# A selective-scan and mixture-of-experts kernel: one tile in four is added into y by a DMA instead of by GpSimd

## The chip, the cores and the metric

The kernel runs on one core of a Trainium2 chip. The time is the device time of one launch in microseconds (us); lower is better. Three runs of the kernel before gave 4412.04, 4418.58 and 4423.32 us, so the median is 4418.58 us.

## The reference, cut to what matters

`x` has the shape (8, 1024, 256). Eight batches go through a bidirectional Mamba block (512 channels, 16 states per channel) and a mixture of experts, each with layer norms and a residual. The change touches the sum over the states:

```
dA = exp(delta[..., None] * A)
bx = delta[..., None] * Bm[:, :, None, :] * x[..., None]
def step(h, inp):
    dAi, bxi, ci = inp
    h = dAi * h + bxi
    return (h, jnp.einsum('ben,bn->be', h, ci))
y = jnp.transpose(ys, (1, 0, 2)) + Dp * x
```

For each time step and channel, `y` is a sum over 16 states `n` of `h_n * c_n`, in each direction, and the two directions are added.

## The kernel before, in words

There are 16 passes `w` (8 batches, two directions), each with 16 states `n`. Per state the kernel handles 4 units of 128 channels x 1024 time steps. For each unit GpSimd makes the drive (`feed_drive`, line 1895, a product of 128x1024), ScalarE makes the decay in two halves of 128x512 (`feed_decay`, line 1610), and VectorE runs two scans of 128x512 into `h` (`scan`, lines 1393 and 1396; line 1384 in the last pass). There are three places for drives and three for decays. GpSimd waits at the semaphore `scanned` until VectorE has emptied the place that it writes next, and can thus be up to three units ahead.

After the four units of a state, TensorE turns `h` into 8 tiles of 128 time steps x 512 channels (`turn_tile`, line 1170, four transposes each) in one of three PSUM buffers `h_t`. A tile `i` is then multiplied by its column of C and summed into `y[:, tb, :]`, where `tb` is its number from 0 to 7. Two ways exist:

- VectorE does both in one instruction (`sum_tile`, line 1405): 1488 tiles.
- ScalarE scales it, and GpSimd adds it. `by_pool` picks the tiles whose number modulo 16 is 2, 6, 10 or 14, one in four. ScalarE writes one of two buffers `scaled` (`scale_tile`, line 1631) and GpSimd adds the buffer into `y` (`pool_tile`, line 1913): 496 tiles. Their `tb` is always 2 or 6, so these two tiles of `y` are only ever touched by ScalarE and GpSimd during a batch.

The first 8 tiles of a batch are written straight into `y` by ScalarE (64 in all), once the DMA that dumps this tile of the batch before (`y_dump`, line 2157, issued by SyncE) has landed. In the last pass the work is cut into two halves of 512 time steps: there 4 tiles per state are summed, so one and the same tile of `y` (first 6, then 2) gets every adding.

The order on each engine is fixed. Time is counted in slots, two per unit; in slot `s` the engines handle their share of a unit, then the tile `s - 8` (GpSimd: `s - 9`), then side work (projections, convolution, norms, experts) from the table `AT`. Side work of GpSimd: `u_mul` (line 1924, 64 products of 128x1024), small norm steps, and in each batch 16 scattering DMAs (line 1970) and 16 gathering DMAs (line 1982), which GpSimd issues itself. All other DMAs are issued by SyncE.

Of the kernel before, what the change touches and what calls it, by code (L numbers as in the profile page):

```python
# [9 lines left out]
ALU = mybir.AluOpType  # L10
# [16 lines left out]
N_SCALED = 2  # L27
# [503 lines left out]
class Plan:  # L531
# [23 lines left out]
    def nth(self, piece, *index):  # L555
        return self.at[piece, index]
# [151 lines left out]
def mamba_moe(nc, x, w_in_t, chan, wx_t, wdt_t, w_out_t, router_w, router_b, w1, b1_t, w2, b2, out):  # L708
# [65 lines left out]
    with ctx:  # L774
        def sb(name, shape):
            return ctx.enter_context(nc.sbuf_tensor(name, shape, F32))

        def sem(name):
            return ctx.enter_context(nc.semaphore(name))
# [23 lines left out]
        scaled = sb("scaled", [P, N_SCALED, ED])  # L803
        conv_diag = sb("conv_diag", [P, TAPS, P])
        y = sb("y", [P, TB, ED])
# [108 lines left out]
        zeros_set = sem("zeros_set")  # L914
        zeros_out = sem("zeros_out")
        tile_scaled = sem("tile_scaled")
        gathered = sem("gathered")
        b_row_in = [sem(f"b_row_in{i}") for i in range(N_B_ROW)]
        y_dumped = [sem(f"y_dumped{i}") for i in range(TB)]
        ew_in = [sem(f"ew_in{i}") for i in range(N_EW + len(wide))]  # L920
# [100 lines left out]
        def state_of(i):  # L1021

            if i < SPLIT * TILES:
                gn, tb = divmod(i, TB)
                return (*divmod(gn, N), tb)
            hs, q = divmod(i - SPLIT * TILES, QB)
            part, n = divmod(hs, N)
            return SPLIT, n, (NH - 1 - part) * QB + q
# [11 lines left out]
        def is_first(i):  # L1040

            return i % (2 * TILES) < TB

        def by_pool(i):
            return i % (2 * TB) in POOL_TILES or is_first(i)

        of_vector = list(accumulate(not by_pool(i) for i in range(NW * TILES)))
        of_pool = list(accumulate(by_pool(i) and not is_first(i) for i in range(NW * TILES)))

        def summed_to(i):  # L1050

            return of_vector[i]

        def pooled_to(i):

            return i + 1 - summed_to(i)

        def gathered_to(i):

            return of_pool[i]  # L1060

        def wait_y(engine, i):

            if i < SPLIT * TILES:
                wait_tile(engine, i - TB)
            elif state_of(i)[1] or i < SPLIT * TILES + QB:
                wait_tile(engine, i - QB)
            else:
                wait_tile(engine, SPLIT * TILES - TB + state_of(i)[2])

        def wait_tile(engine, before):

            if not by_pool(before):
                engine.wait_ge(summed, summed_to(before))
            elif is_first(before):
                engine.wait_ge(tile_scaled, pooled_to(before))
            else:
                engine.wait_ge(gathered, gathered_to(before))

        def ew_place(i):  # L1080

# [271 lines left out]
        def dve_program(dve):  # L1353
# [44 lines left out]
            def sum_tile(i):  # L1398
                w, n, tb = state_of(i)
                b, d = divmod(w, 2)  # L1400
                c_n = c_col[:, w % 2, tb, n:n + 1]
                dve.wait_ge(turned, i + 1)
                dve.wait_ge(done["c_copy"], nth("c_copy", w, NH - 1))
                wait_y(dve, i)
                dve.e.scalar_tensor_tensor(out=y[:, tb, :], in0=h_t[i % N_H_T][:, :], scalar=c_n,  # L1405
                                           in1=y[:, tb, :], op0=ALU.mult, op1=ALU.add).then_inc(summed, 1)
# [186 lines left out]
        def act_program(act):  # L1593
# [23 lines left out]
            def scale_tile(i):  # L1617
                w, n, tb = state_of(i)
                b, d = divmod(w, 2)
                at = gathered_to(i) - 1  # L1620
                act.wait_ge(turned, i + 1)
                act.wait_ge(done["c_copy"], nth("c_copy", w, NH - 1))
                if is_first(i):
                    if b:
                        act.wait_ge(y_dumped[tb], 16 * b)
                    into = y[:, tb, :]
                else:
                    if at >= N_SCALED:
                        act.wait_ge(gathered, at - N_SCALED + 1)
                    into = scaled[:, at % N_SCALED, :]  # L1630
                act.e.mul(into, h_t[i % N_H_T][:, :], c_col[:, w % 2, tb, n:n + 1]).then_inc(tile_scaled, 1)  # L1631

# [239 lines left out]
            for s in range(plan.first, plan.end):  # L1872
                if 0 <= s + N_DECAY - 1 < NH * NU:
                    feed_decay(s + N_DECAY - 1)
                hs, into = divmod(s - 2 * WHOLE - 5, 2 * EC // NH)
                if not into and 0 <= hs < N:
                    keep_h(hs)
                i = s - 2 * EC
                if 0 <= i < NW * TILES and by_pool(i):
                    scale_tile(i)  # L1880
                for piece, index in plan.of("act", s):
                    side_piece(piece, index)


        def pool_program(pool):
# [22 lines left out]
            def pool_tile(i):  # L1908
                tb = state_of(i)[2]
                at = gathered_to(i) - 1  # L1910
                pool.wait_ge(tile_scaled, pooled_to(i))
                wait_y(pool, i)
                pool.e.tensor_tensor(y[:, tb, :], y[:, tb, :], scaled[:, at % N_SCALED, :], ALU.add  # L1913
                                     ).then_inc(gathered, 1)

            def side_piece(piece, index):
                if piece == "u_mul":
# [107 lines left out]
            for s in range(plan.first, plan.end):  # L2025
                k, odd = divmod(s, 2)
                if not odd and 0 <= k + 2 < NU:
                    feed_drive(k + 2)
                i = s - 2 * EC - 1
                if 0 <= i < NW * TILES and by_pool(i) and not is_first(i):  # L2030
                    pool_tile(i)
                for piece, index in plan.of("pool", s):
                    side_piece(piece, index)


        def sp_program(sp):
# [269 lines left out]
            sp.wait_ge(scattered, 16 * TOP * TB * NB)  # L2306
            for k in range(2):
                sp.wait_ge(x_out[k], 16 * NB)
            for tb in range(TB):
                sp.wait_ge(y_dumped[tb], 16 * (NB - 1))  # L2310

# [2 lines left out]
        act_program(Waiter(nc.scalar))  # L2314
        pool_program(Waiter(nc.gpsimd))
        sp_program(Waiter(nc.sync))


# [35 lines left out]
```

## Time and profile before

| | |
|---|---|
| median of 3 runs | 4418.58 us |
| lowest, highest | 4412.04, 4423.32 us |
| span of the profiled execution | 4422.2 us |
| VectorE busy | 3788.5 us (86%) |
| TensorE busy | 3604.0 us (81%) |
| GpSimd busy | 3504.8 us (79%) |
| ScalarE busy | 3101.8 us (70%) |
| bytes moved by DMA | 705.06 MB |

The page gives the profiled execution by its span, from the first to the last instruction; it lies within the three timed runs. An engine counts as busy while an instruction works; issuing a DMA counts as busy on GpSimd in the rows of lines 1970 and 1982, not on SyncE. Groups name the line of the program, the engine, the output and the inputs; "idle before" is the time in which the engine stood still just before them, with what ended it.

### The profile page before, as it was taken

The numbers are of one execution on the slowest core, as the hardware profiler recorded it, in microseconds if no ns is written. First come the engines' busy times: TensorE is split into PE (matmuls) and PEld (weight loads), VectorE is DVE, ScalarE is ACT, GpSimd is POOL, SyncE is SP. The second block draws the span as 40 slices with busy tenths as digits, with TensorE's granted clock in tenths as the row PEclk, the third lists the DMA queues.
The fourth block names the chain that finished last, engine by engine and source line by source line (L and its number), as shares of the span: only waits on it lengthen the run. The fifth ranks groups of instructions, "written<-read, shape, count | busy, mean of one in ns | idle before, by whom it ended". The sixth has DMA issues, their size and how long they took to land.

```text
span 4422.2 us, 57941 instructions
## 1 busy us (share of the span) xinstructions
PE 3604.0 (81%) x18192; PEld 2562.9 (58%) x18192; DVE 3788.5 (86%) x4688; ACT 3101.8 (70%) x5179; POOL 3504.8 (79%) x2085
## 2 busy tenths in 40 slices
PE   4767596888879887798878887798987989788877
PEld 1444454666546655567555774556655665567656
DVE  3999999898998989899898988989999898989710
ACT  4667576787767876688766887678876787668543
POOL 3898887888878888788887888878887888878611
PEclk7878697999979999899879998899998999889988
DMA  6233142556435663357433674345743565336555
GB/s 196 91 107 104 69 150 75 191 183 214 155 104 172 205 210 130 105 182 245 153 124 131 197 238 147 125 151 194 230 141 107 179 220 188 130 113 204 167 167 182
DMA packets 375805, 705.06 MB, mean 159 GB/s; under 512 B 31937, under 2 KB 205514, under 8 KB 371530
## 3 DMA queue, kind: packets, MB, share of 16 engines
q1 hardware_dynamic: 363210, 667.79, 46.0%
q0 software_dynamic: 12288, 33.57, 2.3%
q8 instruction: 145, 2.38, 0.2%
q14 instruction: 162, 1.33, 0.1%
HBM read 529.82 MB, written 171.44 MB: 159 GB/s over the span
## 4 chain that ended last, share of the span: by engine, by line
DVE 29%; PE 25%; POOL 16%; issue 15%; ACT 11%; DMA 3%; SPq 1%; DVEq 0%; POOLq 0%; ACTq 0%
DVE h L1396 10%; POOL drive L1895 9%; DVE h L1393 7%; DVE y L1405 6%; PE h_t L1170 5%; PE side L1204 4%; PE side L1341 4%; PE side L1333 3%; ACT decay L1610 2%; POOL y L1913 2%; POOL xs_dram L1970 2%; DMA expert_w<-in_w 1%; PE side L1318 1%; DVE stats L1450 1%; POOL work L1982 1%
## 5 line engine op out<-in xcount | busy, mean ns | idle before, releaser
L1895 POOL TENSOR_TENSOR drive<-xu,b_row 128x1024 f32<-128x1024 f32 x960 | 2262.7, 2362 | 386.5 <-DVE h L1396 238.8
L1610 ACT ACTIVATE decay<-delta,neg_a 128x512 f32<-128x512 f32 x2048 | 1401.8, 692 | 747.0 <-DVE h L1396 424.5
L1170 PE MATMUL h_t<-ident,h 128*128 128x128 f32 x8192 | 1332.0, 301 | 523.4 <-DVE y L1405 253.4
L1170 PEld LDWEIGHTS h_t<-ident,h 128*128 128x128 f32 x8192 | 1060.1, 155 | 979.1 <-DVE y L1405 373.1
L1405 DVE SCALAR_TENSOR_TENSOR y<-h_t,c_col,y 128x512 f32<-128x512 f32 x1488 | 1085.9, 730 | 54.0 <-PE h_t L1170 52.9
L1913 POOL TENSOR_TENSOR y<-y,scaled 128x512 f32<-128x512 f32 x496 | 631.8, 1274 | 119.4 <-ACT scaled L1631 118.4
L1396 DVE TENSOR_TENSOR_SCAN h<-decay,h,drive 128x512 f32<-128x512 f32 x512 | 654.1, 1278 | 38.6 <-ACT decay L1610 18.6
L1396 DVE TENSOR_TENSOR_SCAN h<-decay,drive 128x512 f32<-128x512 f32 x512 | 622.0, 1215 | 71.9 <-ACT decay L1610 45.8
L1393 DVE TENSOR_TENSOR_SCAN h<-decay,h,drive 128x512 f32<-128x512 f32 x448 | 573.1, 1279 | 44.7 <-ACT decay L1610 23.1
L1393 DVE TENSOR_TENSOR_SCAN h<-decay,drive 128x512 f32<-128x512 f32 x448 | 544.5, 1215 | 76.4 <-POOL drive L1895 55.7
L1204 PE MATMUL side<-prep_work,conv_diag 128*128 128x512 f32 x960 | 460.9, 605 | 27.3 <-DMA prep_work<-xz_dram 19.3
L1631 ACT ACTIVATE scaled<-h_t,c_col 128x512 f32<-128x512 f32 x496 | 334.7, 675 | 76.4 <-PE h_t L1170 76.1
L1333 PE MATMUL side<-xn_t,expert_w 128*128 128x128 f32 x2688 | 354.3, 279 | 26.9 <-DMA expert_w<-in_w 18.0
L1341 PE MATMUL side<-expert_w,work 128*128 128x256 f32 x1304 | 338.7, 408 | 20.7 <-issue 7.8
L1333 PEld LDWEIGHTS side<-xn_t,expert_w 128*128 128x128 f32 x2688 | 325.9, 193 | 40.7 <-issue 19.5
L1341 PEld LDWEIGHTS side<-expert_w,work 128*128 128x128 f32 x1304 | 255.1, 205 | 63.2 <-issue 11.5
L1204 PEld LDWEIGHTS side<-prep_work,conv_diag 128*128 128x128 f32 x960 | 168.7, 194 | 164.0 <-issue 149.6
L1847 ACT ACTIVATE work<-side,b_blocks 128x128 f32<-128x128 f32 x692 | 196.9, 373 | 57.6 <-PE side L1333 57.0
L1982 POOL DMA_INDIRECT work<-ys_dram,slot_i x128 | 123.3, 963 | 143.7 <-DMA ys_dram<-work 112.7
L1924 POOL TENSOR_TENSOR xu<-xu,prep_work 128x1024 f32<-128x1024 f32 x64 | 151.1, 2360 | 60.8 <-DVE prep_work L1436 60.6
L1226 PE MATMUL side<-dbc,wdt_sb 97*128 97x512 f32 x256 | 163.3, 732 | 41.1 <-DVE prep_work L1436 19.3
L1970 POOL DMA_INDIRECT xs_dram<-work,slot_i x112 | 110.7, 989 | 73.5 <-DVE owner_hot L1561 44.0
(205 smaller groups left out, 4355.7 us busy)
## 6 DMA issues: line engine op xcount, KB each, us to landing
expert_w<-in_w SPq DMA_DIRECT2D x350, 512.0 KB, 4.5
b_row<-b_dram SPq DMA_DIRECT2D x240, 512.0 KB, 4.2
x_dram<-xu SPq DMA_DIRECT2D x16, 2048.0 KB, 7.6
delta_dram<-prep_work SPq DMA_DIRECT2D x64, 512.0 KB, 2.9
delta<-delta_dram SPq DMA_DIRECT2D x64, 512.0 KB, 4.9
ys_dram<-work SPq DMA_DIRECT2D x40, 512.0 KB, 6.5
work<-xs_dram SPq DMA_DIRECT2D x38, 512.0 KB, 4.4
h<-in_w SPq DMA_DIRECT2D x34, 512.0 KB, 5.5
```

The source lines that it names most:

```text
L1170: t = pe.e.transpose(h_t[i % N_H_T][:, c * P:(c + 1) * P], its_h[:, c, :], ident[:, :])
L1204: mm = pe.e.matmul(bank[:, :], conv_diag[:, k, :], xz_pad[:, at:at + BANK], start=(k == 0), stop=(k == TAPS - 1))
L1333: mm = pe.e.matmul(bank[:, m * P:(m + 1) * P], wi[:, k, m * P:(m + 1) * P], xn2_t[:, k, at:at + P], start=(k == 0), stop=(k == DC - 1))
L1341: mm = pe.e.matmul(bank[:, q % 2 * D:(q % 2 + 1) * D], h1_blocks(b, G)[:, q, m, :], wo[:, m, :], start=(m == 0), stop=(m == HC - 1))
L1393: return dve.e.tensor_tensor_scan(o[:, ::-1], its_decay[:, ::-1], v[:, ::-1], before, ALU.mult, ALU.add)
L1396: return dve.e.tensor_tensor_scan(o, its_decay, v, before, ALU.mult, ALU.add)
L1405: dve.e.scalar_tensor_tensor(out=y[:, tb, :], in0=h_t[i % N_H_T][:, :], scalar=c_n, in1=y[:, tb, :], op0=ALU.mult, op1=ALU.add).then_inc(s ...
L1610: act.e.activation(decay[:, i % N_DECAY, :], delta[:, c, its], ACT.Exp, scale=neg_a[:, c, w % 2, n:n + 1]).then_inc(decay_made, 1)
L1631: act.e.mul(into, h_t[i % N_H_T][:, :], c_col[:, w % 2, tb, n:n + 1]).then_inc(tile_scaled, 1)
L1895: op = pool.e.tensor_tensor(drive[:, k % N_DRIVE, :], xu[:, w % 2, c, :], b_row[:, row % N_B_ROW, :], ALU.mult)
L1913: pool.e.tensor_tensor(y[:, tb, :], y[:, tb, :], scaled[:, at % N_SCALED, :], ALU.add).then_inc(gathered, 1)
L1970: pool.e.indirect_dma_start(out=xs_dram, out_offset=bass.IndirectOffsetOnAxis(ap=slot_i[:, r, tb:tb + 1], axis=0), in_=tokens_of(b, tb, 1) ...
```

## The change

GpSimd no longer adds the scaled tile. In the same place of its order it issues a DMA from the buffer `scaled` to `y[:, tb, :]` that adds at its destination. The semaphore `gathered`, which counted additions, becomes two semaphores, one for each buffer of `scaled`, and each DMA raises its own by 16 once it has landed. Whoever waited for `gathered` (ScalarE before it writes the buffer again, GpSimd before it adds to the same tile of `y` again, SyncE before it dumps `y`, TensorE before it reads `y` in the last batch) now waits for the landing. At the end SyncE also waits for the last two DMAs.

```
-        gathered = sem("gathered")
+        added = [sem(f"added{i}") for i in range(N_SCALED)]
...
+        def wait_added(engine, at):
+
+            engine.wait_ge(added[at % N_SCALED], 16 * (at // N_SCALED + 1))
...
-                engine.wait_ge(gathered, gathered_to(before))
+                wait_added(engine, gathered_to(before) - 1)
...
-                        act.wait_ge(gathered, at - N_SCALED + 1)
+                        wait_added(act, at - N_SCALED)
...
-                pool.e.tensor_tensor(y[:, tb, :], y[:, tb, :], scaled[:, at % N_SCALED, :], ALU.add
-                                     ).then_inc(gathered, 1)
+                pool.e.dma_start(out=y[:, tb, :], in_=scaled[:, at % N_SCALED, :], accum_op=ALU.add
+                                 ).then_inc(added[at % N_SCALED], 16)
...
+            for i in range(N_SCALED):
+                wait_added(sp, of_pool[-1] - 1 - i)
```

No instruction changes its place. The next two pieces show GpSimd's order in the first batch, where the additions stand among drives and scattering DMAs. Before:

```order
L1895 TENSOR_TENSOR drive<-xu,b_row 128x1024 [waits scanned]
L1913 TENSOR_TENSOR y<-y,scaled 128x512 [waits gathered,tile_scaled]
L1895 TENSOR_TENSOR drive<-xu,b_row 128x1024 [waits scanned] x2
L1913 TENSOR_TENSOR y<-y,scaled 128x512 [waits gathered,tile_scaled]
L1970 DMA xs_dram<-work,slot_i 3072x256 [waits zeros_out,s_slots]
```

After, the same place (the lines are 4 further down):

```order
L1899 TENSOR_TENSOR drive<-xu,b_row 128x1024 [waits scanned]
L1917 DMA y<-scaled 128x512 [waits added1,tile_scaled]
L1899 TENSOR_TENSOR drive<-xu,b_row 128x1024 [waits scanned] x2
L1917 DMA y<-scaled 128x512 [waits added0,tile_scaled]
L1974 DMA xs_dram<-work,slot_i 3072x256 [waits zeros_out,s_slots]
```

The addition has become a DMA that GpSimd issues, and it waits for the landing of an earlier one, where it waited for an earlier addition.

SyncE's order at the end of the first batch, where it dumps `y`. Before:

```order
107 L2157 DMA y_dram<-y 128x512 [waits gathered]
108 L2157 DMA y_dram<-y 128x512 [waits summed] x3
109 L2166 DMA work<-y_dram 128x4x512 [waits y_dumped2,y_dumped3,y_dumped1,y_dumped0]
110 L2157 DMA y_dram<-y 128x512 [waits gathered]
111 L2157 DMA y_dram<-y 128x512 [waits summed]
```

After:

```order
107 L2161 DMA y_dram<-y 128x512 [waits added0]
108 L2161 DMA y_dram<-y 128x512 [waits summed] x3
109 L2170 DMA work<-y_dram 128x4x512 [waits y_dumped2,y_dumped3,y_dumped1,y_dumped0]
110 L2161 DMA y_dram<-y 128x512 [waits added1]
111 L2161 DMA y_dram<-y 128x512 [waits summed]
```

The dumps of the tiles 2 and 6 now wait for a landing; nothing else moved.

## Rows read from the trace of the kernel before

**Rows 1.** Page, part 1: busy time, share of the span, instructions
```profile
PE 3604.0 (81%) x18192; PEld 2562.9 (58%) x18192; DVE 3788.5 (86%) x4688; ACT 3101.8 (70%) x5179; POOL 3504.8 (79%) x2085
```

**Rows 2.** Engines by stage: stage, its length, busy us, clock, DMA share, GB/s
```profile
0.00:110.00 110.00, 48.99 (x100) 19.24 (x101) 37.72 (x58) 52.67 (x79) 41.77 (x89) 0.77 0.66 197
110.00:4164.00 4054.00, 3355.79 (x17161) 2394.06 (x17159) 3713.47 (x4510) 2953.34 (x4889) 3407.41 (x1923) 0.90 0.48 158
4164.00:4422.00 258.00, 199.26 (x933) 149.62 (x932) 37.27 (x121) 95.75 (x211) 55.66 (x75) 0.83 0.50 163
```

**Rows 3.** Page, part 5: groups with busy us, mean ns, idle before
```profile
L1895 POOL TENSOR_TENSOR drive<-xu,b_row 128x1024 f32<-128x1024 f32 x960 | 2262.7, 2362 | 386.5 <-DVE h L1396 238.8
L1405 DVE SCALAR_TENSOR_TENSOR y<-h_t,c_col,y 128x512 f32<-128x512 f32 x1488 | 1085.9, 730 | 54.0 <-PE h_t L1170 52.9
L1913 POOL TENSOR_TENSOR y<-y,scaled 128x512 f32<-128x512 f32 x496 | 631.8, 1274 | 119.4 <-ACT scaled L1631 118.4
L1396 DVE TENSOR_TENSOR_SCAN h<-decay,h,drive 128x512 f32<-128x512 f32 x512 | 654.1, 1278 | 38.6 <-ACT decay L1610 18.6
```

**Rows 4.** Waits: who for whom, total us, times, longest
```profile
DVE h L1396 <- ACT decay L1610: 64.5, 35, 14.6
DVE h L1393 <- POOL drive L1895: 55.7, 23, 8.5
DVE h L1393 <- ACT decay L1610: 43.8, 38, 2.7
DVE h L1396 <- POOL drive L1895: 24.6, 18, 5.3
PE side L1333 <- DMA expert_w<-in_w: 18.0, 19, 2.2
```

**Rows 5.** Page, part 4: the chain that ended last
```profile
DVE h L1396 10%; POOL drive L1895 9%; DVE h L1393 7%; DVE y L1405 6%; PE h_t L1170 5%; PE side L1204 4%; PE side L1341 4%; PE side L1333 3%; ACT decay L1610 2%; POOL y L1913 2%; POOL xs_dram L1970 2%; DMA expert_w<-in_w 1%; PE side L1318 1%; DVE stats L1450 1%; POOL work L1982 1%
```

**Rows 6.** Timeline of GpSimd, 1092 to 1101 us: start, us, instruction, idle before
```profile
1094.53 0.99 POOL L1982 DMA_INDIRECT work<-ys_dram,slot_i  x1 [0.16 <-issue]
1095.82 0.94 POOL L1982 DMA_INDIRECT work<-ys_dram,slot_i  x1 [0.30 <-issue]
1096.79 1.28 POOL L1913 TENSOR_TENSOR y<-y,scaled 128x512 f32<-128x512 f32 x1
1098.23 0.96 POOL L1982 DMA_INDIRECT work<-ys_dram,slot_i  x1 [0.16 <-issue]
1099.50 0.95 POOL L1982 DMA_INDIRECT work<-ys_dram,slot_i  x1 [0.30 <-issue]
1100.47 2.36 POOL L1895 TENSOR_TENSOR drive<-xu,b_row 128x1024 f32<-128x1024 f32 x1
```

**Rows 7.** Line 1982, gathering DMA: duration ns and landing, min/median/max
```profile
L1982 POOL DMA_INDIRECT work<-ys_dram,slot_i x128: 942/948/1051, 1071.7 to 4402.1; - x128
DMA to landing us min/median/max: 2.7/2.8/8.4
```

**Rows 8.** Line 2157, dump of y by DMA: landing, min/median/max
```profile
DMA to landing us min/median/max: 2.0/5.0/9.3
```

**Rows 9.** Timelines of GpSimd and ScalarE, 787 to 795 us
```profile
787.08 1.26 POOL L1913 TENSOR_TENSOR y<-y,scaled 128x512 f32<-128x512 f32 x1
792.92 1.26 POOL L1913 TENSOR_TENSOR y<-y,scaled 128x512 f32<-128x512 f32 x1
794.46 0.67 ACT L1631 ACTIVATE scaled<-h_t,c_col 128x512 f32<-128x512 f32 x1
```

**Rows 10.** Timelines at the end of the first batch: GpSimd, ScalarE
```profile
560.28 1.27 POOL L1913 TENSOR_TENSOR y<-y,scaled 128x512 f32<-128x512 f32 x1
571.27 0.71 ACT L1631 ACTIVATE y<-h_t,c_col 128x512 f32<-128x512 f32 x1
```

**Rows 11.** Timeline of GpSimd at the end of the last pass
```profile
4159.81 1.27 POOL L1913 TENSOR_TENSOR y<-y,scaled 128x512 f32<-128x512 f32 x1 [3.35 <-ACT scaled L1631]
4162.85 1.27 POOL L1913 TENSOR_TENSOR y<-y,scaled 128x512 f32<-128x512 f32 x1 [1.77 <-ACT scaled L1631]
4164.27 0.97 POOL L1982 DMA_INDIRECT work<-ys_dram,slot_i  x1
```

**Rows 12.** Page, part 3: queue: packets, MB, share of 16 engines
```profile
q1 hardware_dynamic: 363210, 667.79, 46.0%
q0 software_dynamic: 12288, 33.57, 2.3%
```

## The prediction

> **What bounds the kernel now.** I read the busy shares first, then the engines by stage, the groups, the waits, the chain and at last the timelines of single places. VectorE is the busiest engine with 3788.5 us [rows 1]. The sum over stages shows where: in the 4054 us from 110 to 4164, in which all scans and tiles lie, it is busy 3713.5 us, or 92%; GpSimd 3407.4 us, 84%; ScalarE 73% [rows 2]. After 4164 us no tile is left, and these 258 us don't change. So VectorE leaves at most 4054 - 3713.5 = 340 us in the middle that anything could win, and only part of it is due to GpSimd: VectorE's scans waited 55.7 + 24.6 = 80.3 us for a drive and 64.5 + 43.8 = 108.3 us for a decay [rows 4]. GpSimd itself stands idle 386.5 us before drives, waiting for scans, and 119.4 us before additions, waiting for ScalarE [rows 3]: mostly it is ahead, and falls behind only in bursts of side work. The chain says the same: of its 4422 us the additions hold 2% [rows 5], about 88 us; at 1.27 us each that is 70 of the 496. The other 426 are hidden behind VectorE, and what they cost can change without moving the end, until GpSimd has no slack left.
>
> **The addition against the DMA's issue.** Removed: 496 additions of 128x512. One occupies GpSimd about 1.25 us: it ends at 1096.79 + 1.28 = 1098.07 [rows 6], and others of its kind are followed by a drive a few hundredths before their written end (mean 1.27) [rows 3]. Added: 496 DMAs issued by GpSimd. Before, GpSimd issues only gathers and scatters of 128 rows. Between two other instructions such a DMA costs its idle and its span, 0.16 + 0.97 = 1.13 us; two in a row, from 1098.07 to 1100.47, cost 2.40 or 1.20 each [rows 6]. The new DMA also has 128 rows, needs no list of rows, but must name its destination for reading as well as for writing. So the price from the rows: nearest 1.13 to 1.20 us; below, nothing but the idle before it, 0.16 us, if the work grows only with the list; above, 2.40 us, if naming the destination twice costs as much as a second DMA. I take 1.15, since the count of rows and the engine are the same. The term: 70 x (1.15 - 1.25) = -7 us. At 0.16 it would be 70 x -1.09 = -76 us, which is near the 80.3 us that VectorE waited for drives in all, its natural limit.
>
> **The landing.** What was done 1.27 us after its start is now done one issue and one landing after it. A gather of 128 KB landed after 2.8 us (2.7 to 8.4) [rows 7], a dump of one tile of y, 256 KB, after 5.0 us (2.0 to 9.3) [rows 8]. The adding DMA moves 256 KB within SBUF and reads the destination too: between 2.0 and 9.3 us, and I take 4.5, nearer to the dump of equal size. Done is thus 1.15 + 4.5 = 5.7 us after the start.
> The Trainium skill (DMA: Bandwidth & Descriptors, "Anatomy of one DMA — SWDGE (gpsimd) path") gives 2.0 us plus bytes / 436e3 for a DMA from this engine; as an estimate 2.6 us here, and by the same formula 2.3 us for the gather, whose row says 2.8. By it, the waits priced below would all vanish.
> Four places wait for it.
> - ScalarE, before it writes the buffer again two tiles later. Behind it in ScalarE's order stand decays. Over all 494 such pairs the shortest distance in the timelines is 7.4 us, and this is one, from 787.08 to 794.46 [rows 9]; the median is 13.1. It holds at 5.7 us: 0.
> - GpSimd, before it adds to the same tile of y. Outside the last pass this lies two tiles back, 11 us or more: 0. In the last pass it is the tile before. Tiles follow at 5.8 us or more, as from 787.08 to 792.92 [rows 9], again just enough, except for the last two, 3.04 us apart [rows 11]. There GpSimd waits 5.7 - 3.0 = 2.7 us, and the gathers of the last batch stand behind it at the head of the tail: +3 us (0 at the shortest landing, +7 at the longest).
> - SyncE, before it dumps tiles 2 and 6, seven times each; behind it stand the next dumps and a row of B. ScalarE needs the dump before it writes the new tile 6: 571.27 - 560.28 = 11.0 us after the addition began [rows 10], and over the seven batch ends this is 10.5 to 16.3 us. Needed are 5.7 + 5.0 = 10.7 us. So about one of the seven is late by tenths: +1 us. With both landings at 9.3 us it would be 7 x up to 9 = 60 us.
> - TensorE, before it turns y in the last batch, more than 10 us later behind other work: 0.
>
> **The DMA engines.** 496 x 0.262 MB = 130 MB more. At the rate of the large queue, 667.79 MB for 46.0% [rows 12], that is 9 points of the 16 engines' time, 18 if the reading of the destination counts like a second copy, on top of 48% [rows 2]. What the kernel waits for DMAs is small: TensorE 18.0 us for expert weights [rows 4], 1% of the chain [rows 5], 44 us. A tenth more on that: +4 us (0 to +12).
>
> **The sum.** -7 + 3 + 1 + 4 = +1 us on 4422 us of the profiled execution, whose span is 3.6 us above the median of the runs. Set against the median of 4418.58 that is 4420; since the DMAs may be a little cheaper than the gathers for want of a list, I say 4419 us, no change. What a measurement of this kernel tells from no change is 0.3%, or 13 us: "same" is 4405 to 4432.
>
> **Rivals.**
> 1. *GpSimd becomes the bound.* The DMA that adds costs more to issue than one that copies. The place is GpSimd's order: it has 386.5 + 119.4 = 506 us of idle, and most of it is not where the bursts are. It turns slower than 4432 once 70 x (cost - 1.25) exceeds 21 us less the +8 of the other terms, so from about 1.45 us. At 1.8 us, the middle between 1.15 and 2.40, the 70 additions on the chain give 70 x 0.55 = 39 us, and about half as many more would join it: 58, with the +8 about 4485 us. At 2.40 us the added 496 x 1.15 = 570 us exceed all its idle; the chain's own 70 give 80 us and the excess 64 more: about 4570 us. For it: two streams of reads instead of one. Against it: 128 rows as before, and the 948 ns of the gathers hardly vary (942 to 1051) [rows 7], which looks like a fixed share.
> 2. *The issue is far cheaper than a gather.* Without a list of rows it takes 0.5 us: 70 x -0.75 = -52 us, +8 for the rest: 4375 us. At 0.8 us: 4396. For it: the list is the only thing that a gather has more. Against it: the 0.30 us of gaps between two gathers don't look like a list.
> 3. *Late landings.* The landing takes 8 us rather than 4.5, with 16 engines already half busy. Then ScalarE stands before the twentieth of its scalings whose distance is under 9.8 us, 25 x about 1 us, in the last pass each of 32 tiles costs up to 3 us while VectorE waits (half of it, 48), and the batch ends cost 7 x 3. Together 25 + 48 + 21, of which I count half as hidden: +47 us and 4460 us. Against it: the medians of the two nearest landings are 2.8 and 5.0 [rows 7, 8], and only single ones reach 8.
> 4. *Descriptors starve.* In this case the largest gather span is 1051 ns against 942 at the least [rows 7], so a collision with VectorE costs 0.1 us at most; on 70 DMAs 7 us, 4427 us.
> The Trainium skill (SBUF — State Buffer, "Who interferes with whom") states that a VectorE instruction in a two-port mode locks GpSimd out of writing descriptors altogether. The rows bear out no lock here, so this rival keeps a small chance.
>
> **How the numbers follow.** Forecast, issue near 1.15 us and landing under 6 us: 0.42. Rival 1: 0.24. Rival 2: 0.22. Rival 3: 0.08. Rival 4: 0.04. Faster by over 0.3%: nearly all of rival 2 and a little of the forecast, 0.25. Slower: rivals 1 and 3 and a little of the forecast, 0.34. Same: 0.41. The likeliest case by itself has 4408 to 4432. The range that should hold 8 in 10 reaches into both sides: 4375, where rival 2 takes 0.5 us, and 4500, beyond rival 1 at 1.8 us; left out are an issue near nothing and one near 2.4 us.
>
> **What would show it.** Right: GpSimd's group of the adding DMAs with a mean near 0.95 us, starts of the next instruction 1.1 to 1.2 us after, landings of 4 to 5 us, VectorE's waits for drives still near 80 us, the DMA share up by 9 to 18 points with TensorE's wait for expert weights below 30 us. Wrong: a span of 1.5 us or more, with VectorE's waits for drives in the hundreds (rival 1); a span near 0.5 us (rival 2); new waits of ScalarE's scaling or GpSimd's issue for the landing (rival 3). A time under 4375 us would mean that the additions held VectorE back in a way that its waits for drives don't show.

## The result

The changed kernel takes 4461.32 us (median of 4 runs, 4456.50 to 4470.96) against 4420.95 us for the kernel before, measured beside it: the ratio is 1.0098, with an interval from 1.0079 to 1.0117. By the ratio it is slower by about 43 us (the two medians lie 40 us apart), more than the 0.3% that can be told from no change. In the experiments below one run of the kernel with every second tile took 4951.65 us at a lower clock (0.71) and is left out. The forecast was 4419 us; the time lies inside the range of 4375 to 4500 us, but in the case to which 0.34 was given, "slower", and not in the one with 0.41, "same". Of the signs that the prediction named for being right, waits for expert weights below 30 us are the one that clearly failed.

### The profile page after: what moved, and what is told of

Its sections match the earlier page's. It is cut to its first block, busy times and chain, and to the rows that moved or that the text cites. A ratio compares the mean times of both kernels' runs of the same rounds, so it can differ in the third digit from the quotient of the medians.

```text
span 4464.2 us, 57942 instructions
## 1 busy us (share of the span) xinstructions
PE 3613.4 (81%) x18192; PEld 2569.1 (58%) x18192; DVE 3781.4 (85%) x4688; ACT 3102.0 (69%) x5179; POOL 3347.7 (75%) x2085
## 3 DMA queue, kind: packets, MB, share of 16 engines
q1 hardware_dynamic: 363210, 667.79, 46.2%
q0 software_dynamic: 83712, 163.63, 19.1%
## 4 chain that ended last, share of the span: by engine, by line
PE 28%; DVE 28%; issue 13%; ACT 12%; POOL 9%; DMA 8%; SPq 1%; DVEq 0%; POOLq 0%; ACTq 0%
DVE h L1400 10%; DVE h L1397 6%; DVE y L1409 6%; PE h_t L1174 6%; POOL drive L1899 4%; PE side L1345 4%; PE side L1208 4%; DMA expert_w<-in_w 4%; PE side L1337 3%; ACT decay L1614 3%; POOL xs_dram L1974 2%; PE side L1302 1%; DVE stats L1454 1%; PE side L1245 1%; PE side L1322 1%
## 5 line engine op out<-in xcount | busy, mean ns | idle before, releaser
L1899 POOL TENSOR_TENSOR drive<-xu,b_row 128x1024 f32<-128x1024 f32 x960 | 2353.2, 2491 | 506.9 <-DVE h L1400 299.8
L1397 DVE TENSOR_TENSOR_SCAN h<-decay,h,drive 128x512 f32<-128x512 f32 x448 | 572.6, 1278 | 46.2 <-ACT decay L1614 24.4
L1917 POOL DMA_DIRECT2D y<-scaled x496 | 469.8, 947 | 175.3 <-ACT scaled L1635 140.2
L1337 PE MATMUL side<-xn_t,expert_w 128*128 128x128 f32 x2688 | 358.1, 280 | 48.2 <-DMA expert_w<-in_w 43.1
L1986 POOL DMA_INDIRECT work<-ys_dram,slot_i x128 | 126.4, 987 | 149.5 <-DMA ys_dram<-work 116.2
L1905 POOL TENSOR_TENSOR drive<-xu,b_row 128x1024 f32<-128x1024 f32 x64 | 158.9, 2563 | 29.7 <-DVE h L1388 21.2
```

Source lines behind the costliest of these rows:

```text
L1337: mm = pe.e.matmul(bank[:, m * P:(m + 1) * P], wi[:, k, m * P:(m + 1) * P], xn2_t[:, k, at:at + P], start=(k == 0), stop=(k == DC - 1))
L1397: return dve.e.tensor_tensor_scan(o[:, ::-1], its_decay[:, ::-1], v[:, ::-1], before, ALU.mult, ALU.add)
L1899: op = pool.e.tensor_tensor(drive[:, k % N_DRIVE, :], xu[:, w % 2, c, :], b_row[:, row % N_B_ROW, :], ALU.mult)
L1917: pool.e.dma_start(out=y[:, tb, :], in_=scaled[:, at % N_SCALED, :], accum_op=ALU.add).then_inc(added[at % N_SCALED], 16)
```

## The profile after

Busy times of the page, which answer to [rows 1]:

```profile
PE 3613.4 (81%) x18192; PEld 2569.1 (58%) x18192; DVE 3781.4 (85%) x4688; ACT 3102.0 (69%) x5179; POOL 3347.7 (75%) x2085
```

GpSimd has 157 us less to do than before and VectorE as much as before, yet the span is 42 us longer (4422.2 and 4464.2 us). By stage (columns as in [rows 2]; the last tile now ends at 4206 us):

```profile
110.00:4206.00 4096.00, 3365.56 (x17169) 2400.41 (x17167) 3707.86 (x4512) 2955.46 (x4893) 3252.54 (x1925) 0.90 0.67 188
4206.00:4464.00 258.00, 199.17 (x930) 150.14 (x930) 37.28 (x121) 95.15 (x209) 54.49 (x73) 0.82 0.49 163
```

The tail is 258 us as before. All of the loss lies in the middle, 4096 us in place of 4054. The granted clock is 0.90 in both. What moved is the last column but one, the share of the DMA engines' time: 0.48 to 0.67. The queues say who took it, against [rows 12]:

```profile
q1 hardware_dynamic: 363210, 667.79, 46.2%
q0 software_dynamic: 83712, 163.63, 19.1%
```

The queue of GpSimd's DMAs went from 2.3% to 19.1%, 16.8 points for 130 MB, while the large queue moves five times as much in 46.2%. The groups that answer to [rows 3]:

```profile
L1899 POOL TENSOR_TENSOR drive<-xu,b_row 128x1024 f32<-128x1024 f32 x960 | 2353.2, 2491 | 506.9 <-DVE h L1400 299.8
L1409 DVE SCALAR_TENSOR_TENSOR y<-h_t,c_col,y 128x512 f32<-128x512 f32 x1488 | 1083.2, 728 | 84.3 <-PE h_t L1174 83.0
L1917 POOL DMA_DIRECT2D y<-scaled x496 | 469.8, 947 | 175.3 <-ACT scaled L1635 140.2
```

GpSimd now stands idle longer before drives (506.9 us against 386.5) and before the tiles (175.3 against 119.4): it is less of a limit than it was. VectorE's own additions wait for TensorE's turned tiles instead, 83.0 us against 52.9. The waits (who for whom: us, times, longest), which answer to [rows 4]:

```profile
DVE y L1409 <- PE h_t L1174: 83.0, 110, 3.6
DVE h L1400 <- ACT decay L1614: 75.4, 39, 15.1
DVE h L1397 <- ACT decay L1614: 50.5, 38, 3.3
DVE h L1397 <- POOL drive L1899: 49.4, 20, 5.2
DVE h L1400 <- POOL drive L1899: 22.7, 14, 5.1
PE side L1337 <- DMA expert_w<-in_w: 43.1, 37, 2.8
PEld side L1345 <- DMA expert_w<-in_w: 9.9, 9, 2.4
PE side L1345 <- DMA expert_w<-in_w: 7.6, 7, 2.2
POOL y L1917 <- DMA y<-scaled: 16.0, 8, 4.7
ACT y L1635 <- DMA y_dram<-y: 4.5, 3, 2.4
```

VectorE waits less for drives (72.1 us, 80.3 before) and more for decays and turned tiles. That ScalarE and TensorE both fall behind because TensorE waits for its loads is my reading of these rows. Its waits for expert weights are 60.6 us in these three rows, 20.1 us before, of which [rows 4] show the largest, 18.0. (A weight load and the matmul behind it can each have a row for the same wait; sums of this kind compare kernels and are not lost time.) The chain, which answers to [rows 5]:

```profile
DVE h L1400 10%; DVE h L1397 6%; DVE y L1409 6%; PE h_t L1174 6%; POOL drive L1899 4%; PE side L1345 4%; PE side L1208 4%; DMA expert_w<-in_w 4%; PE side L1337 3%; ACT decay L1614 3%; POOL xs_dram L1974 2%; PE side L1302 1%; DVE stats L1454 1%; PE side L1245 1%; PE side L1322 1%
```

The loads of expert weights hold 4% of it (1% before) and the additions have left it. How late they are stands in the DMA issues (size, median us from issue to landing), of the kernel before and then of the changed one:

```profile
expert_w<-in_w SPq DMA_DIRECT2D x350, 512.0 KB, 4.5
b_row<-b_dram SPq DMA_DIRECT2D x240, 512.0 KB, 4.2
delta<-delta_dram SPq DMA_DIRECT2D x64, 512.0 KB, 4.9
```

```profile
expert_w<-in_w SPq DMA_DIRECT2D x350, 512.0 KB, 5.2
y<-scaled POOLq DMA_DIRECT2D x496, 256.0 KB, 5.6
b_row<-b_dram SPq DMA_DIRECT2D x240, 512.0 KB, 4.9
delta<-delta_dram SPq DMA_DIRECT2D x64, 512.0 KB, 6.0
```

The same loads land 0.7 to 1.1 us later. One stretch in which experts are computed, before and after (columns as in [rows 2]):

```profile
1300.00:1600.00 300.00, 264.13 (x1471) 196.98 (x1469) 269.07 (x298) 234.63 (x402) 253.42 (x135) 0.96 0.60 198
```

```profile
1300.00:1600.00 300.00, 259.92 (x1448) 193.42 (x1447) 265.82 (x297) 233.03 (x397) 237.21 (x134) 0.96 0.79 228
```

Where the DMA engines were busy 60% on the mean they are now at 79%, and the trace has 1448 matmuls in these 300 us where it had 1471. (The changed kernel is some microseconds behind by then, so the stretch doesn't hold quite the same work.)

## The experiments

Three theories at first. **A**: the adding DMAs take time on the 16 DMA engines, the loads that TensorE waits for land later. **B**: the waits for the adding DMA's own landing. **C**: the issue costs GpSimd more than its span says, by disturbing the drives beside it. Each ratio below is against the kernel before, run on the same chip.

**Only the bytes taken away.** The changed kernel, all 496 DMAs at their places, each moving 16 of the 512 columns (the rest of the tile isn't added):

```diff
-                pool.e.dma_start(out=y[:, tb, :], in_=scaled[:, at % N_SCALED, :], accum_op=ALU.add
+                pool.e.dma_start(out=y[:, tb, 0:16], in_=scaled[:, at % N_SCALED, 0:16], accum_op=ALU.add
```

> The changed kernel, but each adding DMA moves only 16 of the 512 columns (the other columns of these tiles aren't summed). Its issue on GpSimd, its 128 rows and every wait for a landing stay; nearly all of the bytes go. Theory A (the transfers take time of the 16 DMA engines from the expert weights): the loss goes and what GpSimd's cheaper instruction gives is left, 4395 to 4420 us, TensorE's wait for expert weights back at about 20 us, DMA share below 52% in the middle. Theory B (waits for landings): the landing still takes some 2 to 3 us of fixed time, so half or more of the loss stays, 4440 us or more. Theory C (issuing a DMA disturbs GpSimd's drives, whose mean rose from 2362 to 2491 ns): the loss stays whole, about 4460 us, with the drives' mean near 2490 ns.

Measured: 4406.44 us, ratio 0.9977 (0.9969 to 0.9986). The issues are as long as in the full kernel (median 879 and 881 ns), and the drives too (mean 2483 and 2491 ns). So C falls: with the whole price of the issue paid, the kernel is 10 us faster than with the additions. Waits for expert weights are 19.2 us, as before. The 53 us between this kernel and the changed one (by the two ratios) are the bytes', with the longer landings that they bring.

**The bytes kept, the adding taken away.** The changed kernel, the DMA copies the tile over y (so these tiles aren't summed):

```diff
-                pool.e.dma_start(out=y[:, tb, :], in_=scaled[:, at % N_SCALED, :], accum_op=ALU.add
+                pool.e.dma_start(out=y[:, tb, :], in_=scaled[:, at % N_SCALED, :]
```

> The changed kernel, with the adding DMA turned into one that copies the same 256 KB (the tile of y is overwritten, so the sum over states is left out for these tiles). Theory A: a packet of 2 KB takes about 84 ns instead of 178, the share of this queue falls from 19 to about 10%, and about half of the loss goes: 4430 to 4445 us, TensorE's wait for expert weights 30 to 45 us. Theory B: the landing gets shorter by under 1 us and the loss stays near 4455. Theory C: the same, near 4460 us.

Measured: 4408.06 us, ratio 0.9983 (0.9974 to 0.9992), waits for expert weights 35.4 us. That is faster than all three theories said: A had left half of the loss, 4430 to 4445 us. Each semaphore wait for a landing is still in the program, but GpSimd spends only 4.8 us in them here against 16.0, so this kernel speaks against B as the main cause and doesn't price those 16 us. The queue:

```profile
q0 software_dynamic: 51968, 163.63, 10.0%
```

The same 163.63 MB take 10.0% in place of 19.1%. Adding makes them take 16.8 points where a copy takes 7.7. It also changes the issue, as GpSimd's timeline of this kernel shows (start, us, instruction):

```profile
1110.58 0.60 POOL L1917 DMA_DIRECT2D y<-scaled  x1
1111.19 4.69 POOL L1899 TENSOR_TENSOR drive<-xu,b_row 128x1024 f32<-128x1024 f32 x2
1115.81 0.58 POOL L1917 DMA_DIRECT2D y<-scaled  x1
1116.40 4.70 POOL L1899 TENSOR_TENSOR drive<-xu,b_row 128x1024 f32<-128x1024 f32 x2
```

The same place in the changed kernel:

```profile
1113.01 1.05 POOL L1917 DMA_DIRECT2D y<-scaled  x1
1113.64 5.14 POOL L1899 TENSOR_TENSOR drive<-xu,b_row 128x1024 f32<-128x1024 f32 x2
1118.26 1.40 POOL L1917 DMA_DIRECT2D y<-scaled  x1
1118.85 5.50 POOL L1899 TENSOR_TENSOR drive<-xu,b_row 128x1024 f32<-128x1024 f32 x2
```

And in the kernel before:

```profile
1107.55 1.26 POOL L1913 TENSOR_TENSOR y<-y,scaled 128x512 f32<-128x512 f32 x1
1108.77 4.68 POOL L1895 TENSOR_TENSOR drive<-xu,b_row 128x1024 f32<-128x1024 f32 x2
1113.42 1.26 POOL L1913 TENSOR_TENSOR y<-y,scaled 128x512 f32<-128x512 f32 x1
1114.65 4.66 POOL L1895 TENSOR_TENSOR drive<-xu,b_row 128x1024 f32<-128x1024 f32 x2
```

Read these from the start of the first tile's instruction to the end of the fourth drive, less the four drives' 9.34 us: before 1119.31 - 1107.55 - 9.34 = 2.42, or 1.21 us for an addition; adding DMA 11.34 - 9.34 = 2.00, or 1.00 each; copying DMA 10.52 - 9.34 = 1.18, or 0.59 each. That is one place. An adding DMA lets the next drive begin after 0.6 us, and the spans then overlap: the first pair of drives ends at 1118.78, the next DMA starts at 1118.26. Over the whole execution GpSimd's busy time, in which an overlap counts once, fell by 3504.8 - 3347.7 = 157.1 us, 0.32 us for each of the 496, and by 3504.8 - 3178.2 = 326.6 us, 0.66 us each, with the copy. Taken from 1.21 that makes 0.89 us for an adding DMA and 0.55 for a copying one, so the cost of an adding DMA is an estimated 0.9 to 1.0 us, about what its span says.

**Only the load on the engines added.** The kernel before, with a copy of 512 KB from SBUF to a spare DRAM tensor issued by ScalarE at each of the 496 tiles:

```diff
+                if not is_first(i):
+                    if at:
+                        act.wait_ge(spare_out, 16 * at)
+                    act.e.dma_start(spare_dram[at % 2], w_in_sb[:, 0, :]).then_inc(spare_out, 16)
```

> The kernel before, additions on GpSimd as they were, and beside each of the 496 ScalarE issues a DMA of 512 KB (4 KB rows) from a constant in SBUF to DRAM, which no computing waits for except ScalarE's next such issue. It takes about 1.3 us of each of the 16 engines, near the 1.5 us of an adding DMA. Theory A: slower than the kernel before by 20 to 60 us, 4440 to 4480, with TensorE's wait for expert weights at 45 us or more. Theories B and C: GpSimd and all landings in the sum are as before, so only ScalarE's own issues cost, under 15 us: 4420 to 4435 us.

Measured: 4460.48 us, ratio 1.0115 (1.0097 to 1.0132). Waits for expert weights 43.3 us, their landing 5.2 us. The additions are all on GpSimd here, and the loss of the change is there nevertheless. By the ratio that is 51 us. ScalarE's own time for the issues is part of it, so the size alone proves little; a later kernel does without it.

**What GpSimd's time in these places is worth.** The kernel before with each addition cut to 16 columns (the rest isn't added), 221 ns in place of 1272:

```diff
-                pool.e.tensor_tensor(y[:, tb, :], y[:, tb, :], scaled[:, at % N_SCALED, :], ALU.add
+                pool.e.tensor_tensor(y[:, tb, 0:16], y[:, tb, 0:16], scaled[:, at % N_SCALED, 0:16], ALU.add
```

> The kernel before, with each addition on GpSimd cut to 16 of 512 columns (the others aren't summed for these tiles). It shows what GpSimd's time in these 496 places is worth at most. By the chain of the kernel before (additions 2%, 70 of 496 on it) and VectorE's 80 us of waits for drives: 30 to 80 us faster, 4340 to 4390 us. The alignment of the two traces, in which stretches with scattering DMAs won 1 to 4 us each and others nothing, says less: 10 to 30 us faster.

Measured: 4384.77 us, ratio 0.9934 (0.9922 to 0.9946): -32 us by the medians (24 to 34 by the interval) for -1.05 us at each. It counts as if 31 of the 496 stood on the path (23 to 33), not 70. Nothing that replaces the additions can win more than about 32 us and a little.

**Where the loss arises.** In the next three, part of the tiles is added by the DMA and part by GpSimd as before; expert weights are loaded in stretches between those of gathers, scatters and norms. The place of a tile decides (208 tiles in the quiet stretches, 288 in the others), and every wait goes to the semaphore that its tile raises. These kernels and the last three below have one more difference: to free a semaphore, VectorE's convolution steps count on the one of its routing steps. The kernel with 16 columns in the quiet stretches has it too and is not slower than the kernel before, so it doesn't make the losses.

```diff
+        def by_dma(i):
+            return 20 <= (i + 9) % 256 < 125
...
+                if by_dma(i):
+                    pool.e.dma_start(out=y[:, tb, :], in_=scaled[:, at % N_SCALED, :], accum_op=ALU.add
+                                     ).then_inc(added[at % N_SCALED], 16)
+                else:
+                    pool.e.tensor_tensor(y[:, tb, :], y[:, tb, :], scaled[:, at % N_SCALED, :], ALU.add
+                                         ).then_inc(gathered, 1)
```

> 208 of the 496 tiles, those of the stretches in which no expert weights are loaded, are added by the DMA; the other 288 by GpSimd's addition as in the kernel before. Theory A (the adding DMAs take time on the 16 DMA engines, expert weights land later and TensorE waits for them): almost none of the loss is here, and the cheaper issue is kept: ratio to before 0.996 to 1.000 (4400 to 4417 us), TensorE's waits for expert weights near 20 us as before. Rival D (each adding DMA costs the same wherever it stands, 41/496 = 0.08 us): ratio 1.004, 4434 us. Rival B (waits for the landing): 1.002 to 1.004, with new waits of ScalarE or GpSimd for the DMA.

Measured: 4429.96 us, ratio 1.0036 (1.0021 to 1.0051). A miss for theory A as I had worded it (0.996 to 1.000): the price that D gave, with waits for expert weights at 19.2 us as A had them. The complement has `not` before the condition:

> The complement: 288 of the 496 tiles, those of the stretches in which expert weights are loaded, are added by the DMA; the other 208 by GpSimd. Theory A: all of the loss or more (the changed kernel also gained in the quiet stretches): ratio 1.009 to 1.013, 4457 to 4475 us, TensorE's waits for expert weights near 60 us. Rival D: 288/496 of the loss, ratio 1.0055, 4441 us, waits in proportion.

Measured: 4451.90 us, ratio 1.0076 (1.0063 to 1.0089), waits for expert weights 62.0 us. This lies between A (1.009 to 1.013) and D (1.0055), and meets neither. The stretches with expert weights carry the larger part, by the ratios 0.12 us for each DMA against 0.08 in the quiet ones (0.05 in the repetition below), but not all of it. In the stretch from 1300 to 1600 us the DMA engines are busy 77% in this kernel and 61% in the quiet one, against 60% before and 79% in the changed kernel. Half the tiles at all places, `state_of(i)[2] == 6`:

> Every second of these tiles (tile 6 of each state) is added by the DMA, tile 2 by GpSimd: half the DMA traffic at all places. If the loss is linear in the traffic: ratio 1.005 (4438 us), waits for expert weights near 40 us. If it sets in only above a certain load of the DMA engines, as the plain copy with half the engine time and no loss suggests: ratio 0.998 to 1.001 (4408 to 4421 us), waits for expert weights 20 to 30 us.

Measured: 4429.57 us, ratio 1.0030 (1.0020 to 1.0040), waits for expert weights 31.1 us (profiled in its fastest run, 4416.7 us): between the two expectations, a third of the loss for half the traffic. And all tiles with half the columns (256 of 512 added):

> The changed kernel with each of the 496 adding DMAs cut to 256 of the 512 columns (the rest of the tile isn't added). Theory A: the loss goes with the time on the DMA engines; their queue's share should come out between the 5.1% of the DMA of 16 columns and the 19.1% of the full one, near 12%; between the ratios 0.998 (copy without adding, 10.0%) and 1.010 (19.1%): 1.000 to 1.003, 4417 to 4430 us. Rival E (an adding DMA disturbs by its kind, whatever its size, once it is of some hundred bytes a row): as the full one, 1.008 or more. Waits for expert weights 25 to 40 us by A, near 60 by E.

Measured: 4420.18 us, ratio 1.0003 (0.9994 to 1.0013), 12.1% for the queue as expected, waits for expert weights 31.9 us. E falls for this size.

**Adding against mere occupation.** The changed kernel, each DMA a plain copy of twice the bytes to DRAM (the tile isn't added):

```diff
-                pool.e.dma_start(out=y[:, tb, :], in_=scaled[:, at % N_SCALED, :], accum_op=ALU.add
-                                 ).then_inc(added[at % N_SCALED], 16)
+                pool.e.dma_start(spare_dram[at % 2], w_in_sb[:, 0, :]).then_inc(added[at % N_SCALED], 16)
```

> In the changed kernel each of the 496 adding DMAs is replaced by a plain copy, from the same engine at the same place, of 512 KB from SBUF to a spare DRAM tensor (so these tiles aren't added into y). Nothing is added by a DMA, but the DMA engines are as occupied as by the adding ones: the 512 KB writes of an earlier run took 12.9 points of the 16 engines' time, the adding DMAs 16.8. Theory A (it is the time on the DMA engines, whatever fills it): ratio 1.006 to 1.012, 4443 to 4470 us, expert weights waited for 40 to 60 us. Rival E (adding is special, a plain DMA of any size is harmless, as that of 256 KB was): 0.997 to 1.001, 4404 to 4421 us.

(The 12.9 points named there for the 512 KB writes of ScalarE's queue are too low; its row has 15.2%.) Measured: 4460.53 us, ratio 1.0098 (1.0080 to 1.0117), the changed kernel's own ratio. Its queue and its waits:

```profile
q0 software_dynamic: 83712, 293.65, 17.1%
```

```profile
PE side L1338 <- DMA expert_w<-in_w: 40.1, 36, 3.0
PEld side L1346 <- DMA expert_w<-in_w: 11.9, 11, 2.1
PE side L1346 <- DMA expert_w<-in_w: 9.0, 10, 1.9
```

That is 61.0 us against the changed kernel's 60.6. No byte is added, the issue is cheaper, and the loss is the same: E falls, A stands.

**Why the quiet stretches lose too.** The 208 quiet DMAs with 16 columns (the rest not added), and beside them the full ones again:

```diff
-                    pool.e.dma_start(out=y[:, tb, :], in_=scaled[:, at % N_SCALED, :], accum_op=ALU.add
+                    pool.e.dma_start(out=y[:, tb, 0:16], in_=scaled[:, at % N_SCALED, 0:16], accum_op=ALU.add
```

> The 208 tiles outside the stretches with expert weights are added by a DMA of 16 of the 512 columns, the other 288 by GpSimd in full; so the same issues as in the kernel with full DMAs there (ratio 1.0036), without their bytes. If traffic costs time there too, through transfers other than the expert weights (gathers, scatters, rows that TensorE waits for): ratio 0.997 to 1.000. If the loss there comes from the issue itself or from how additions and DMAs alternate on GpSimd: 1.002 to 1.004.

> The kernel with full DMAs for the 208 quiet tiles once more, beside its thin version: ratio 1.002 to 1.005 if the first value holds; near 1.000 if that was chance. TensorE's waits for DMAs other than expert weights, 110 us against 89 before in its first profile, show again if they are the cause.

Measured: thin 4413.20 us, ratio 0.9989 (0.9978 to 0.9999); full again 4428.95 us, ratio 1.0025 (1.0012 to 1.0037). The first value holds, and the bytes make it, 16 us on the same chip. The waits of the thin kernel:

```profile
PEld side L1332 <- DMA work<-ys_dram,slot_i: 25.3, 12, 7.1
PE side L1332 <- DMA work<-ys_dram,slot_i: 20.4, 11, 6.7
PE side L1338 <- DMA work<-xs_dram: 17.3, 2, 15.0
```

And of the full one, in its second profile:

```profile
PEld side L1332 <- DMA work<-ys_dram,slot_i: 31.8, 15, 7.1
PE side L1332 <- DMA work<-ys_dram,slot_i: 25.5, 12, 6.7
PE side L1338 <- DMA work<-xs_dram: 19.9, 2, 14.4
```

What is late there is the gathered and the routed rows, not the weights (the rows for expert weights sum to 22.9 us in the thin kernel and 17.7 in the full one). Whether such rows are fetched late or take longer isn't settled: the gather's own landing keeps its median of 2.8 us in the changed kernel. Summed over all rows in which TensorE (matmuls and weight loads) waits for any DMA: 111.6 us thin, 127.7 and 130.6 full.

**A version that might beat both.** DMAs only for the 36 additions that stand in an unbroken stretch of GpSimd's work at whose end VectorE waited for a drive in the kernel before; the other 460 on GpSimd:

```diff
+        def by_dma(i):
+            return of_pool[i] - 1 in BURSTS
```

> Only the 36 additions that lie in a stretch of unbroken work of GpSimd at whose end VectorE waited for a drive in the kernel before are made by the DMA, the other 460 by GpSimd. Theory A: nearly the whole gain of the cheaper issue, hardly any traffic (1.2 points): ratio 0.996 to 0.999, 4399 to 4413 us, VectorE's waits for drives below 80 us. If the issue isn't cheaper where it matters: 1.000 +- 0.0015.

Measured: 4419.88 us, ratio 1.0000 (0.9990 to 1.0010). No gain, where theory A had said 0.996 to 0.999: 36 times 0.21 to 0.32 us would have been 8 to 12 us at the very most. In these places the issue also lasts longer, 998 ns on the median against 881 in the changed kernel. And though VectorE's waits for drives fell, to 50.5 + 14.2 = 64.7 us on the lines that had 80.3, the end did not move. Of all versions that compute the whole result none beats the kernel before.

All together. "Share" is that of the DMA engines from 110 to 4150 us; "TensorE waits" is the sum of its waits for any DMA; "against before" is by the ratio; the last column, an estimate, takes out what GpSimd wins, by the rates above (10 us for 496 adding issues and in proportion for fewer, 31 x (1.21 - 0.59) = 19 us for copying ones):

| kernel | share | TensorE waits, us | against before, us | left for the traffic, us |
|---|---|---|---|---|
| before | 0.48 | 110.2 | | |
| 16 columns | 0.51 | 104.6 | -10 | 0 (by definition) |
| full, 208 quiet tiles (again) | 0.57 (0.56) | 130.6 (127.7) | +16 (+11) | 20 (15) |
| copy, 256 KB | 0.57 | 128.0 | -8 | 11 |
| every second tile | 0.57 | 126.4 | +13 | 18 |
| full, the other 288 tiles | 0.58 | 144.4 | +34 | 40 |
| 256 columns | 0.60 | 125.7 | +1 | 11 |
| before + ScalarE's 512 KB | 0.64 | 149.4 | +51 | 51, with ScalarE's issues |
| copy, 512 KB | 0.65 | 175.7 | +43 | 62 |
| changed kernel | 0.66 | 176.6 | +43 | 53 |

The intervals of the ratios reach 4 to 8 us to either side. Where the DMAs are spread over the whole kernel, the loss isn't in proportion to the load: up to 0.60 it is 11 to 18 us, at 0.64 to 0.66 it is 51 to 62. The waits for DMAs tell it the same way: up by 16 to 18 us, and then by 39 to 66. The mean share over the kernel is no ruler by itself, though: the 288 tiles among the expert weights cost 40 us at 0.58. The two parts of the tiles, 34 and 11 to 16 us, add up to about the whole loss of 43, whereas half of the traffic at every place costs a third of it; so what counts is how dense the traffic is in a stretch.

## Why the prediction was right or wrong

The sum was +1 us and the measurement is +43 us. By its steps:

- **The issue, -7 us.** Right in its result. The span was forecast as near 0.95 us and is 0.947 on the mean; the cost of an adding DMA is 0.9 to 1.0 us and not 1.15, that of an addition 1.21 and not 1.25; and not 70 but about 31 count. 31 x 0.21 = 7 us, or 31 x 0.32 = 10 us by GpSimd's busy time over the whole execution, and the kernel of 16 columns measures 10 (6 to 14). The two errors cancelled: "70 additions on the chain" read the chain's share as if each of its members were worth its whole time; that another engine's work lies close behind each is argued, not shown.
- **Rival 1**, GpSimd as the bound: false. Its idle before drives grew, from 386.5 to 506.9 us.
- **Rival 2**, an issue of 0.5 us: false for the adding DMA. It is what a copying one costs (0.59), and even that won only 8 us with its traffic.
- **The landing.** 5.6 us on the median (3.3 to 10.0) against my 4.5:

```profile
L1917 POOL DMA_DIRECT2D y<-scaled x496: 841/881/1952, 129.8 to 4203.0; - x166
DMA to landing us min/median/max: 3.3/5.6/10.0
```

- **Its four waits.** ScalarE waits for no adding DMA before it writes the buffer again: 0, as forecast. GpSimd waits 16.0 us in eight places, where 3 us were forecast for the last one; the copy of 256 KB has 4.8 us of such waits and is faster than before, that of 512 KB has 10.7 and loses as much as the changed kernel. Their own price wasn't separated; it is 16 us of the 43 at the very most. The dump of y makes ScalarE wait three times, 4.5 us, against one batch end and 1 us. TensorE none. Errors of this size don't decide the sum. The Trainium skill (DMA: Bandwidth & Descriptors, "Anatomy of one DMA — SWDGE (gpsimd) path") led to an estimate of 2.6 us for this landing; the measured 5.6 us decide against it for an adding DMA of this size beside such traffic. Nor would all waits have vanished by that estimate: 1.15 + 2.6 us is still 0.7 us more than the 3.04 us between the last two tiles.
- **Rival 3**, late landings, named 4460 us, which is the time measured, by a mechanism that is not there: landings of 8 us and ScalarE held up before 25 of its scalings. A right number for a wrong reason; its own sum, half of 94 us on top of the forecast, gives some 4463 to 4466 us besides.
- **Rival 4**, descriptors starved by VectorE: the longest issue is 1952 ns, but the median 881, and the kernel of 16 columns with the same issues (up to 1932 ns) is faster than before. No more than the spread of a few.
- **The DMA engines, +4 us (0 to +12): the step that failed.** The share itself was bounded rightly, 9 to 18 points, and came out at 16.8, at the end where the reading of the destination counts like a second copy. What was wrong is the sentence "A tenth more on that". It took the wait of the kernel before, 44 us on the chain, and let it grow by a tenth, for which it gave no reason; 9 to 18 points on 48 are a fifth to two fifths, and even in that proportion the term would have been only 8 to 16 us. But a wait is what is left when a lead is used up. TensorE's loads of expert weights came nearly in time before: with a landing of 4.5 us, 19 matmuls of the first row waited 18.0 us. At 5.2 us, 15% later, 37 wait 43.1 us, and all three rows together three times as long as before; other loads that I had not priced, the gathered and routed rows, come on top. Measured, the term is +53 us, the waits for the adding DMAs' own landings within it. No rival held it, because I priced the load of the DMA engines only as a share of the whole kernel, 48% and 9 to 18 points more, and not stage by stage: from 1300 to 1600 us it goes from 0.60 to 0.79.

What is shown: that the bytes' time on the DMA engines makes the loss (16 columns against 512; 512 KB copies without any adding), that it arises mostly, not only, where expert weights are loaded, and that, with the DMAs spread evenly, it grows faster than the load. What is argued only: that each late load costs by using up its lead. A test would have been to load the weights one tile earlier; it wasn't tried.

## What to carry to other kernels

Before work is moved from an engine to a DMA, look at the DMA share in the very stretch (0.60 here, before the change), and at how late the loads already are there: where an engine already waits for loads in many places, as for 19 of them here, price each new point of share by the waits that it opens and not by the bytes. Count an adding DMA as two copies of its size, as this case measured it (24.2 against 11.0 us of DMA-engine time), and ask how much of the engine's time that it frees is worth anything: cut the work to a stub first (here -32 us for all of it), for that is the most that any replacement can bring. A share of the chain is not that number.

## What was not expected of the hardware

- An adding DMA of 256 KB within SBUF took 24.2 us of DMA-engine time (16.8% of 16 x 4464.2 us over 496), a plain one 11.0 us (7.7% of 16 x 4410.5), one of half the columns 14.0 (9.8% of 16 x 4418.9), a plain one of 512 KB to DRAM 21.3 (14.8% of 16 x 4455.8).
- Its issue on GpSimd is longer whatever its size: median 881 ns with 512 columns, 879 with 256 and with 16, against 577 ns for the plain copy of 256 KB and 578 for that of 512 KB.
- The next instruction of GpSimd starts 0.6 us after an adding DMA's start and overlaps its span, but drives then last 2491 ns on the mean, against 2362 before and 2363 beside plain copies. Their spans overlap the next instruction's too, so not all of that is cost.
- Gathers of 128 KB in the same queue landed after 2.8 us on the median as before, at 19.1% of that queue as at 2.3%, while loads of 512 KB from SyncE's queue went from 4.5 to 5.2 us.
